# Mixing a batch's low-rank rows in one step, and correcting h and logits with one 272-column matmul a tile

## The reference, cut to what matters

```
x = x + L0(x)     # x W0' + 0.5 (x A0[label0[b]]) B0'
x = x + L1(x)     # x (quantised (W1 + delta) + delta)'
x = x + L2(x)     # x W2' + 0.5 (x A2[label2[b]]) B2'
x = x + L3(x)     # base x W3'; logits x Wr' + 5 onehot(label7[b]); top 2, softmax -> gates
                  # + 2 * sum_e gate_e * (x A3_e') B3_e'
```

## Time and profile before

| | |
|---|---|
| median of 3 runs | 607.87 us (607.7 to 608.03) |
| profiled execution | 607.86 us |
| its span | 606.1 us |
| PE busy | 600.0 us, 99% |
| DVE busy | 391.9 us, 65% |
| ACT busy | 214.4 us, 35% |
| granted TensorE clock | 1.0 throughout |
| batches 1 to 7 start at | 394.52 us and then every 29.8 to 29.9 us |

### The profile page before, as it was taken

One profiled execution on the slowest core, in us unless ns is written; L12 is line 12 of the kernel. 1 busy time (PEld: TensorE's weight loads), 2 busy tenths in 40 slices (PEclk: granted clock), 3 DMA queues, 4 the chain that ended last, 5 costly groups with the idle time before them and its releaser, 6 DMA issues.

```text
span 606.1 us, 9230 instructions
## 1 busy us (share of the span) xinstructions
PE 600.0 (99%) x3247; PEld 536.4 (89%) x3247; DVE 391.9 (65%) x727; ACT 214.4 (35%) x403; POOL 79.7 (13%) x111
## 2 busy tenths in 40 slices
PE   8999999999999999999999999999999999999998
PEld 7999999899999999888888788788888888888887
DVE  3488998999989829200004598967474747475653
ACT  3434233346233129211111278433333333333330
POOL 2101010023000000000000005040404040303120
PEclk9999999999999999999999999999999999999999
DMA  9963220362000030200001110222131313030301
GB/s 263 263 164 92 100 72 1 43 199 89 1 1 1 1 36 1 45 1 0 0 0 35 40 30 1 50 91 79 60 88 50 96 43 109 30 121 17 101 4 71
DMA packets 57824, 37.69 MB, mean 62 GB/s; under 512 B 26684, under 2 KB 51516, under 8 KB 57796
## 3 DMA queue, kind: packets, MB, share of 16 engines
q1 hardware_dynamic: 57796, 37.31, 22.2%
HBM read 28.91 MB, written 8.39 MB: 62 GB/s over the span
## 4 chain that ended last, share of the span: by engine, by line
PE 90%; DVE 7%; ACT 2%; DMA 1%; issue 0%; POOL 0%; POOLq 0%
PE acc L1414 48%; PE acc L1551 29%; PE acc L1572 4%; PE aux L1401 2%; DVE q L1041 2%; PE acc L1574 2%; DVE qtmp L1040 1%; PE acc L1580 1%; PE acc L1581 1%; PE aux L1489 1%; DVE w_lo L945 1%; DVE hg_lo L952 1%; DMA g<-in_L_cond_W_dram 1%; PE acc L1401 1%; ACT hg_hi L611 1%
## 5 line engine op out<-in xcount | busy, mean ns | idle before, releaser
L1414 PE MATMUL acc<-hg_hi,w_hi 128*128 128x352 f32 (+2 forms) x384 | 87.2, 335 | 1.3 <-DVE w_lo L945 0.9
L1414 PE MATMUL acc<-hg_lo,w_hi 128*128 128x352 f32 (+2 forms) x384 | 85.8, 331 | 0.0
L1414 PE MATMUL acc<-hg_hi,w_lo 128*128 128x352 f32 (+2 forms) x384 | 85.6, 330 | 0.0
L1414 PEld LDWEIGHTS acc<-hg_hi,w_hi 128*128 128x128 f32 x384 | 66.3, 188 | 2.9 <-DVE w_lo L945 1.3
L1414 PEld LDWEIGHTS acc<-hg_hi,w_lo 128*128 128x128 f32 x384 | 67.3, 188 | 0.0
L1414 PEld LDWEIGHTS acc<-hg_lo,w_hi 128*128 128x128 f32 x384 | 67.2, 188 | 0.0
L945 DVE TENSOR_TENSOR w_lo<-a_t,w_hi 128x1024 fp32r<-128x1024 f32 (+2 forms) x9 | 9.9, 1105 | 82.1 <-ACT w_hi L603 82.1
L1041 DVE TENSOR_TENSOR q<-q,qtmp 128x1024 f32<-128x1024 f32 x48 | 59.5, 1240 | 1.7
L768 ACT CAST left_hi<-xr 128x512 fp32r<-128x512 f32 x64 | 39.6, 622 | 51.1 <-PE acc L1551 33.6
L539 POOL TENSOR_TENSOR xr<-xr 128x512 f32<-128x512 f32 x28 | 35.7, 1298 | 130.4 <-DVE left_lo L1190 129.1
L1551 PE MATMUL acc<-rh_a,left_hi 128*128 128x512 f32 (+1 forms) x132 | 52.7, 399 | 0.0
(11 more groups left out here) (213 smaller groups left out, 1042.5 us busy)
## 6 DMA issues: line engine op xcount, KB each, us to landing
x_st<-in_x_dram SPq DMA_DIRECT2D x64, 128.0 KB, 2.9
out_dram<-part SPq DMA_DIRECT2D x31, 256.0 KB, 2.8
g<-in_L_cond_W_dram SPq DMA_DIRECT2D x8, 512.0 KB, 7.2
w_st<-in_L_cond_W_dram SPq DMA_DIRECT2D x8, 512.0 KB, 4.6
a_t<-in_L_cond_weight_dram SPq DMA_DIRECT2D x8, 512.0 KB, 5.0
w_raw<-in_L_cond_weight_dram SPq DMA_DIRECT2D x8, 512.0 KB, 4.3
a_raw<-in_L_cond_lora_A_dram SPq DMA_DIRECT2D x5, 128.0 KB, 3.6
a_raw<-in_L_cond_lora_A_dram SPq DMA_DIRECT2D x20, 32.0 KB, 1.9
```

The costliest lines, as they stand in the source:

```text
L1414: last = pe.matmul(acc[0:a.shape[-1], slot, bank * BANK:bank * BANK + c1 - c0], a[:, k, :], b[:, k, c0:c1], start=(at == 0 and n == 0), st ...
```

## The change

Batches 1 to 7 (not first): the rows of both tiles lie side by side in `vt` and `vm` (128 x 2 x 128), `mix` runs once on both (two matmuls of 256 columns instead of four of 128), `m_high` and `m_low` run once on 256 columns, and both `correct_others` stand behind the W product. `turn_g(0)` moves from the third block of X = S2·T2 to the middle of Z = S1·T1, `turn_g(1)` one block later. All batches: the correction tables are `vbe`, high and low side by side, so `correct_others` is one matmul of 272 columns whose low half goes to the second half of the E bank; therefore the h and logit columns of that half are copied to SBUF only after the correction (`copy_h` on ACT), and `best_two` waits for that copy instead of for the matmul. On DVE `left_low S1` and `m_low` come ahead of `best_two(0)`, and `g_low(0)` ahead of `left_low S4`. Before the first batch the split of `vb` is done in two pieces on ACT and DVE.

```diff
-        vb_hi, vb_lo = place("vb_hi", 79616, [P, C_LOW2], F32R), place("vb_lo", 205824, [P, C_LOW2], F32R)
+        vb_hi, vb_lo = place("vb_hi", 79616, [P, D], F32R), place("vb_lo", 205824, [P, D], F32R)
+        vbe = place("vbe", 34752, [P, 2, NR], F32R)
-        vm = [place(f"vm{h}", 37888 + 512 * h, [P, P], F32R) for h in range(2)]
+        vm = place("vm", 37888, [P, 2, P], F32R)
 ...
+        AUX_MIX = aux[:, P:3 * P]
+        AUX_GATED = (aux[:, BANK + 2 * P:BANK + 3 * P], aux[:, 3 * P:4 * P])
 ...   (ACT, ahead of the first batch)
             def vb_high(half):
-                act.copy(vb_hi[half * 2 * R:(half + 1) * 2 * R, :], bp[:, 0:C_LOW2]).then_inc(vb_hd, 1)
+                rows = slice(half * 2 * R, (half + 1) * 2 * R)
+                act.copy(vb_hi[rows, :], bp[:, 0:D]).then_inc(vb_hd, 1)
+                act.copy(vbe[rows, 0, :], bp[:, D:C_LOW2]).then_inc(vb_hd, 1)
 ...   (ACT)
-                    act.copy(hl[h][:], E_BANK[h][:, E_W:]).then_inc(second_copied, 1)
+                    act.copy(hl[h][:, 0:EH], E_BANK[h][:, E_W:E_W + EH]).then_inc(second_copied, 1)
+
+                def copy_h(h):
+                    act.wait_ge(r_done, b * 2 + (h + 1))
+                    act.copy(hl[h][:, EH:], E_BANK[h][:, E_W + EH:]).then_inc(h_copied, 1)
 ...   (ACT, batches 1 to 7)
                 left_high(b, "S2")
-                m_high(0)
                 v_high(1)
                 done("M2")
                 left_high(b, "S1")
-                m_high(1)
+                m_high()
+                copy_h(0)
+                copy_h(1)
                 exponential(0)
 ...   (DVE)
                 def best_two(h):
-                    dve.wait_ge(r_done, b * 2 + (h + 1))
+                    dve.wait_ge(h_copied, b * 2 + (h + 1))
 ...   (DVE, batches 1 to 7)
                 left_low(b, "S2")
-                m_low(0)
                 v_low(1)
+                left_low(b, "S1")
+                m_low()
                 best_two(0)
-                m_low(1)
                 gated(0)
-                left_low(b, "S1")
                 best_two(1)
+                g_low(0)
                 left_low(b, "S4")
                 gated(1)
-                g_low(0)
 ...   (PE)
                 def correct_others(h):
-                    at = E_BANK[h][:, EH:E_W]
-                    pe.matmul(at, vm[h][:], vb_hi[:, D:C_LOW2], start=False, stop=False, skip_group_check=True)
-                    pe.matmul(at, vm[h][:], vb_lo[:, D:C_LOW2], start=False, stop=True,
-                              skip_group_check=True).then_inc(r_done, 1)
+                    at = E_BANK[h].rearrange("p (u c) -> p u c", u=2)[:, :, EH:]
+                    pe.matmul(at, vm[:, h], vbe[:], start=False, stop=True, skip_group_check=True).then_inc(r_done, 1)
 ...
                 product("Y", "A12", "B21", range(1), start=True)
-                mix(0)
+                if first:
+                    mix(0)
                 product("Y", "A12", "B21", range(1, 2))
                 turn_v(1)
                 product("Y", "A12", "B21", range(2, HALF)).then_inc(step_done, 1)
-                correct_others(0)
                 if first:
+                    correct_others(0)
 ...
                 product("W", "A22", "T4", range(1), start=True)
                 mix(1)
                 product("W", "A22", "T4", range(1, HALF)).then_inc(step_done, 1)
+                if not first:
+                    correct_others(0)
                 correct_others(1)
 ...
-                product("Z", "S1", "T1", range(HALF), start=True).then_inc(step_done, 1)
+                product("Z", "S1", "T1", range(2), start=True)
+                if not first:
+                    turn_g(0)
+                product("Z", "S1", "T1", range(2, HALF)).then_inc(step_done, 1)
```

More of the change, by code:

```diff
@@ L250, in aux_at, with gated_at @@
             return aux[:, h * BANK + n * P:h * BANK + (n + 1) * P]
+        AUX_MIX = aux[:, P:3 * P]
+        AUX_GATED = (aux[:, BANK + 2 * P:BANK + 3 * P], aux[:, 3 * P:4 * P])
+        def gated_at(first, h):
+            return aux_at(h, 2) if first else AUX_GATED[h]
         w3_in = [sem(f"w3_in{k}") for k in range(KT)]
@@ L582, in _ @@
             pool.wait_ge(eyed, 2)
-            pool.wait_ge(vb_done, 5)
+            pool.wait_ge(vb_done, 6)
             mixer(first_l2)
@@ L1262, in v_low, with m_low @@
                     dve.wait_ge(v_hd, b * 2 + (h + 1))
-                    dve.tensor_tensor(vt[2 * R:], aux_at(h, 0)[2 * R:], vt[2 * R:].bitcast(F32),
+                    dve.tensor_tensor(vt[2 * R:, h], aux_at(h, 0)[2 * R:], vt[2 * R:, h].bitcast(F32),
                                       ALU.subtract).then_inc(v_split, 1)
[L1266 to L1269, removed]
+                def m_low(h=None):
+                    if first:
+                        dve.wait_ge(m_hd, h + 1)
+                        low, mixed = vm[2 * R:, h], aux_at(h, 1)
+                    else:
+                        dve.wait_ge(m_hd, b + 2)
+                        low, mixed = vm[2 * R:].rearrange("p h r -> p (h r)"), AUX_MIX
+                    dve.tensor_tensor(low, mixed[2 * R:], low.bitcast(F32), ALU.subtract).then_inc(m_split, 1)
                 def g_low(h):
                     dve.wait_ge(g_hd, b * 2 + (h + 1))
-                    dve.tensor_tensor(hgt_l[h][:], aux_at(h, 2), hgt_h[h][:].bitcast(F32),
+                    dve.tensor_tensor(hgt_l[h][:], gated_at(first, h), hgt_h[h][:].bitcast(F32),
                                       ALU.subtract).then_inc(g_split, 1)
@@ L1579, in finish @@
                     cols, at = slice(half * HD + c.start, half * HD + c.stop), BANKS[bank][:, c]
-                    pe.matmul(at, vm[h][:], vb_hi[:, cols], start=False, stop=False, skip_group_check=True)
-                    pe.matmul(at, vm[h][:], vb_lo[:, cols], start=False, stop=False, skip_group_check=True)
+                    pe.matmul(at, vm[:, h], vb_hi[:, cols], start=False, stop=False, skip_group_check=True)
+                    pe.matmul(at, vm[:, h], vb_lo[:, cols], start=False, stop=False, skip_group_check=True)
                     three(at, (hgt_h[h][:], hgt_l[h][:]), (b3_hi[half][:, c], b3_lo[:, cols]),
@@ L1587, in turn_v, with mix @@
                     turn_tile(aux_at(h, 0), v_sb[:].rearrange("p u c -> p (u c)")).then_inc(v_tr, 1)
-                def mix(h):
-                    pe.wait_ge(v_split, b * 2 + (h + 1))
+                def mix(h=None):
+                    pe.wait_ge(v_split, h + 1 if first else b * 2 + 2)
                     pe.wait_ge(tsel_ready, b * 2 + 2)
-                    pe.matmul(aux_at(h, 1), tsel_h[:], vt[:], start=True, stop=False, skip_group_check=True)
-                    pe.matmul(aux_at(h, 1), tsel_l[:], vt[:], start=False, stop=True,
-                              skip_group_check=True).then_inc(mix_done, 1)
+                    at, rows = (aux_at(h, 1), vt[:, h]) if first else (AUX_MIX, vt[:].rearrange("p h r -> p (h r)"))
+                    pe.matmul(at, tsel_h[:], rows, start=True, stop=False, skip_group_check=True)
+                    pe.matmul(at, tsel_l[:], rows, start=False, stop=True, skip_group_check=True).then_inc(mix_done, 1)
                 def correct_others(h):
-                    pe.wait_ge(m_split, b * 2 + (h + 1))
+                    pe.wait_ge(m_split, h + 1 if first else b + 2)
                     if first:
-                        pe.wait_ge(vb_hd, 4)
-                        pe.wait_ge(vb_done, 5)
-                        pe.wait_ge(vb_zero, 1)
-                    at = E_BANK[h][:, EH:E_W]
-                    pe.matmul(at, vm[h][:], vb_hi[:, D:C_LOW2], start=False, stop=False, skip_group_check=True)
-                    pe.matmul(at, vm[h][:], vb_lo[:, D:C_LOW2], start=False, stop=True,
-                              skip_group_check=True).then_inc(r_done, 1)
+                        pe.wait_ge(vb_hd, 6)
+                        pe.wait_ge(vb_done, 6)
+                        pe.wait_ge(vb_zero, 2)
+                    at = E_BANK[h].rearrange("p (u c) -> p u c", u=2)[:, :, EH:]
+                    pe.matmul(at, vm[:, h], vbe[:], start=False, stop=True, skip_group_check=True).then_inc(r_done, 1)
                 def turn_g(h):
                     pe.wait_ge(hg_ready, b * 2 + (h + 1))
-                    turn_tile(aux_at(h, 2), hg[:].rearrange("p e r -> p (e r)")).then_inc(g_tr, 1)
+                    turn_tile(gated_at(first, h), hg[:].rearrange("p e r -> p (e r)")).then_inc(g_tr, 1)
                 def wait_left(name):
@@ L1658, in pair @@
                 product("X", "S2", "T2", range(3))
-                turn_g(0)
+                if first:
+                    turn_g(0)
                 product("X", "S2", "T2", range(3, HALF)).then_inc(step_done, 1)
@@ L1672, in pair @@
                 pe.wait_ge(part_copied, count(b, COPIES, "M6"))
-                product("X", "S3", "T3", range(1))
+                turn_at = 1 if first else 2
+                product("X", "S3", "T3", range(turn_at))
```

(2 more changed lines are left out.)

30 lines of the change are left out of this document (18 added, 12 removed).

## The result

| | before | changed |
|---|---|---|
| median of 4 runs | 607.79 us (607.62 to 608.03) | 615.65 us (615.35 to 616.21) |
| ratio | | 1.013, 95% interval 1.0113 to 1.0148 |
| profiled span | 606.1 us | 614.1 us |
| PE, DVE busy | 600.0, 391.9 us | 600.7, 391.1 us |
| granted TensorE clock | 1.0 | 1.0 |

The account below looks back on a forecast made before the run. PE was taken to bound the kernel, with DVE's gapless chain making it wait: 607.86 + 0.55 (batch 0) + 8.1 (batches 1 to 6) - 0.39 (batch 7) = 616.1 us, range 613.0 to 618.3.

Parts of the forecast that it names:

- batch 0: First batch: the split of vb and best_two(0) waiting for copy_h make it 0.55 us longer, bounds 0 and 0.9.
- batch 7: Last batch: no x_turn, sel_low or left_low A12 ahead of g_low(1), so no wait; it gains 0.39 us.
- finish of W starts: PE's end of the W product waits for g_low(1): offset 24.7 instead of 23.3, a 1.4 us wait.
- out C22 ends: DVE's output step behind x_turn(b,1,1), awaited by the next batch's first product: ends at offset 31.0.
- The move of the correction: correct_others(0) goes from behind Y to behind W: best_two(0) starts 3.05 us later, x_turn(b,0,1) 2.0 later.
- Two waits in a row, the second ruling: PE waits at the finish of W, then for out C22, which sets batches 1 to 6: 31.15 us for 29.82.
- PE's saving: Merged matmuls save 0.20 us in mix and 0.19 in correct_others: 0.39 a batch, 0.19 in batch 0.
- The output in two pieces: The 272-column correction writes two pieces of a bank: put at 0.127 us, bounds 0.12 and 0.22.
- The 81 ns at 128 columns: Skill's figure for small matmuls, not used: about 0.2 us less saved a batch, some 1.5 over the kernel.
- The room at the finish of Y: g_low(0) on DVE ends at offset 19.0 for PE's finish of Y at 19.3; such rooms 0.2 to 0.5 us.

Follow-up runs that it names:

- The early correction: Changed kernel with mix right behind Y, both corrections behind W's second block, m_high and m_low ahead of left S1: 613.75 us; with turn_g(0) and turn_g(1) earlier too, 608.21 us.
- the correction alone: Against the kernel before: corrections as one matmul of 272 columns with copy_h, at their old places, one mix per tile, old orders: 608.18 us, ratio 1.0013.

## Why the prediction was right

The time (615.65 for 616.1) and the steps that make it up agree. Of the 8.0 us between the spans (614.1 - 606.1), batch 0 has 0.49, batches 1 to 6 have (581.69 - 395.01) - (573.32 - 394.52) = 7.88 for 8.1 forecast, and batch 7 has -0.37, so the sum is not right by errors that cancel. Offsets in batch 3, from 457.49:

| step | forecast | measured |
|---|---|---|
| best_two(0) starts | 14.05 | 471.51: 14.02 |
| x_turn(b,0,1) starts | 21.2 | 478.73: 21.24 |
| g_low(1) ends | 24.55 | 482.00: 24.51 |
| finish of W starts | 24.7 | 482.16: 24.67 |
| out C22 ends | 31.0 | 488.36: 30.87 |
| next batch starts | 31.15 | 488.52: 31.03 |
| batch, mean of six | 31.15 | 186.61 / 6 = 31.10 |

- **The move of the correction** was named as the large term. The move without the merging shows it: the same positions with the old matmuls and no copy_h give 616.28 us. The early correction, with turn_g moved along, shows the reverse: all merged, and 608.21. What the prediction had not seen is that the move makes the chain late at two places. In the changed kernel turn_g(0) costs nothing, since g_low(0) starts at 476.23 without a wait for it; but once the correction is early, the late turn_g(0) by itself still holds the kernel at 613.75.
- **Two waits in a row, the second ruling.** Shown by the three kernels that take away one, the other and both: 616.56, 614.15 and 605.89 us, from 615.65. A reader of one wait's length, 10.0 us in the list, would have expected 606 from the first of them.
- **Batch 0**: 0.55 forecast. From its first matmul to batch 1's, 394.52 - 363.69 = 30.83 before and 395.01 - 363.69 = 31.32 after: 0.49. With copy_h(0) ahead of left_high S1 it is 394.48 - 363.44 = 31.04, so 0.28 of it was that copy's place, as forecast (0.3).
- **Batch 7** gained 0.37, for 0.39 forecast: 606.1 - 573.32 = 32.78 before; after, 614.1 - 581.69 = 32.41.
- **PE's saving was mis-sized.** 0.39 a batch was forecast. The merged mix and its two large neighbours take 469.04 - 468.35 = 0.69 us, what each of the two old mixes took, so one whole pair of 0.235 is saved; the corrections likewise take 0.24 for both tiles, what one pair took. A matmul of 128 columns thus cost 0.117 and not the 0.11 of the sum. The two pairs are 0.47, and the batch without waits is 0.5 shorter (29.31 for 29.82). The forecast hardly felt this, because in batches 1 to 6 the saving is inside the wait. The output in two pieces costs nothing that can be seen: two corrections fill 470.88 to 471.12, 0.12 each.
- **The 81 ns at 128 columns** of the Trainium skill (TensorE: Matmul & The Clock Gate, Back-to-back issue gap) would have made the saving smaller. The trace doesn't agree: 128 columns take 117 ns here, and the measured saving, 0.5 a batch, is larger than my own sum.
- **The room at the finish of Y** was in the prediction as 0.2 to 0.5 us. That was too much, since it left out the 0.17 us from DVE's end to PE's start, which the prediction itself uses for the finish of W. In the changed kernel g_low(0) ends at 476.52 for a finish at 476.71, which leaves 0.02 us: that no wait was added there was luck. With the correction in its old place the room was 0.16 and was used up, and the correction alone was mis-forecast for this reason. In the same way I had not seen that g_low(0), moved ahead on DVE, turns a late turn_g(0) into a wait for all that is queued behind it.

## What to carry to other kernels

An engine that is busy for 60% of a batch can still set the batch's length: read its timeline from the step that a move makes later to the next appointment with the bounding engine, add up the starts, and compare with the room at each appointment, not with its idle time in the batch. When two waits stand in a row behind one late chain, removing either gives next to nothing and the list of waits then names the other; take the chain's start or both ends. Merging two small steps into one means waiting for the later of the inputs, so the merge pays only if what depends on the earlier one has that much room, or is moved as well: here 0.5 us a batch was saved and 1.8 us lost, until the order behind it was changed.

## What the runs showed of the hardware

- An appointment that DVE just misses costs PE more than the time by which it is missed: the finish effectively starts 0.16 to 0.17 us after the end of the DVE instruction, in batch 0 before and at 482.16 in the changed kernel, and the first two matmuls are 0.33 to 0.34 apart in place of 0.23. In these kernels an appointment is kept only if DVE ends that much earlier.
- A matmul of 256 or 272 columns here took 0.12 us from start to start, and a pair of 128 columns as much as a pair of 256 (0.235 with the loose spacing around it): 128 columns cost no less than 256 here.
- The landing of x stays about 6 us behind the transpose that empties its buffer wherever that transpose stands: 6.22 us before (473.43 to 479.65), 5.95 after (478.73 to 484.68), 6.27 in the early correction with turn_g moved along (474.35 to 480.62), each in batch 3.
